# Sampling distances of a deformable convolution made by GpSimd instead of VectorE

## What is computed

```
out = conv2d(x, conv1_w, conv1_b); out = relu(batchnorm(out, ...))
offset = conv2d(out, off_w, off_b)              # 18 maps: y and x for 9 taps
py = off[:, :, 0] + ky + oy;  px = off[:, :, 1] + kx + ox
sampled = v00*w00 + v01*w01 + v10*w10 + v11*w11   # bilinear, zero outside the image
out = einsum('bckhw,ock->bohw', sampled, w) + b
```

## Time and profile before

| | us |
|---|---|
| median of 3 runs (lowest, highest) | 107.54 (107.26, 108.07) |
| the profiled execution | 107.54 |
| its span, first to last instruction | 105.4 |
| PE busy in the span | 93.1 (88%) |
| DVE busy | 68.5 (65%) |
| ACT busy | 48.4 (46%) |
| POOL busy | 29.9 (28%) |
| products on DVE (line 666), 21 instructions | 20.9 |

### The profile page before, as it was taken

One profiled execution on the slowest core, in us unless ns is written; L12 is line 12 of the kernel. 1 busy time (PEld: TensorE's weight loads), 2 busy tenths in 40 slices (PEclk: granted clock), 3 DMA queues, 4 the chain that ended last, 5 costly groups with the idle time before them and its releaser, 6 DMA issues.

```text
span 105.4 us, 3065 instructions
## 1 busy us (share of the span) xinstructions
PE 93.1 (88%) x1280; PEld 67.1 (64%) x1280; DVE 68.5 (65%) x186; ACT 48.4 (46%) x96; POOL 29.9 (28%) x43
## 2 busy tenths in 40 slices
PE   5979995796496999999978899999999999996970
PEld 2346641485375777777733889989899745583940
DVE  6655974239999998399335455655556569759451
ACT  5655812308989999756526990000000015651120
POOL 3000916910000004999880000000000006285510
PEclk9999999999999999999999999999999999999999
DMA  2899999999100000000000000000000000000001
GB/s 72 233 346 382 213 190 202 200 191 217 50 3 6 0 0 3 6 0 0 0 6 0 0 6 0 6 0 6 0 6 0 0 6 3 0 0 6 0 0 50
DMA packets 4589, 6.35 MB, mean 60 GB/s; under 512 B 512, under 2 KB 3840, under 8 KB 4576
## 3 DMA queue, kind: packets, MB, share of 16 engines
q1 hardware_dynamic: 4576, 6.16, 24.9%
HBM read 6.03 MB, written 0.13 MB: 58 GB/s over the span
## 4 chain that ended last, share of the span: by engine, by line
PE 70%; DVE 17%; DMA 4%; ACT 3%; issue 3%; SPq 1%; DVEq 0%; ACTq 0%
PE ps L1041 23%; PE ps L961 13%; PE ps L972 8%; DVE st L666 6%; PE ps L854 5%; DMA taps<-in_taps 4%; PE ps L1156 3%; PE ps L834 3%; PE ps L1054 2%; PE ps L913 2%; DVE hats L643 1%; PE ps L898 1%; DVE prodt L790 1%; PE ps L1149 1%; PE ps L1088 1%
## 5 line engine op out<-in xcount | busy, mean ns | idle before, releaser
L666 DVE TENSOR_TENSOR st<-hats 128x1024 f32<-128x1024 f32 (+1 forms) x21 | 20.9, 1043 | 2.2 <-PE ps L961 2.2
L961 PE MATMUL ps<-ident,st 128*128 128x128 f32 x144 | 17.9, 276 | 2.3 <-DVE st L666 2.3
L507 ACT ACTIVATE s<-ps 128x512 f32<-128x512 f32 x33 | 17.3, 601 | 4.5 <-PE ps L961 4.5
L961 PEld LDWEIGHTS ps<-ident,st 128*128 128x128 f32 x144 | 15.6, 141 | 5.9 <-DVE st L666 3.4
L834 PE MATMUL ps<-zeros 128*128 128x512 bf16 x53 | 13.9, 413 | 1.9 <-DVE zeros L576 1.2
L439 ACT ACTIVATE std<-mv,par 128x1 f32<-128x1 f32 x4 | 1.2, 295 | 27.4 <-DVE mv L564 27.4
L1041 PE MATMUL ps<-yt,wband 128*64 128x96 f32 (+1 forms) x240 | 12.3, 259 | 0.5 <-DVE yt L700 0.5
L1041 PEld LDWEIGHTS ps<-yt,wband 128*64 128x64 f32 x240 | 11.4, 136 | 1.5 <-issue 0.7
L1041 PE MATMUL ps<-ytb,wband 128*64 128x96 f32 (+1 forms) x240 | 12.2, 259 | 0.1
L1041 PEld LDWEIGHTS ps<-ytb,wband 128*64 128x64 f32 x240 | 11.3, 136 | 0.9 <-DVE ytb L715 0.2
L834 PEld LDWEIGHTS ps<-zeros 128*128 128x128 bf16 x53 | 5.2, 104 | 8.6 <-issue 1.9
(11 more groups left out here) (177 smaller groups left out, 121.6 us busy)
## 6 DMA issues: line engine op xcount, KB each, us to landing
wband<-in_wb SPq DMA_DIRECT2D x4, 720.0 KB, 14.5
wa<-in_wa SPq DMA_DIRECT2D x1, 576.0 KB, 7.0
taps<-in_taps SPq DMA_DIRECT2D x1, 560.0 KB, 5.1
taps<-in_taps SPq DMA_DIRECT2D x1, 448.0 KB, 4.0
wa<-in_wa SPq DMA_DIRECT2D x1, 324.0 KB, 5.4
wc<-in_wc SPq DMA_DIRECT2D x1, 256.0 KB, 15.5
cst<-in_cst SPq DMA_DIRECT2D x1, 242.0 KB, 5.4
sel<-in_sel SPq DMA_DIRECT2D x1, 192.0 KB, 4.3
```

Source lines behind the costliest of these rows:

```text
L507: a.activation(s[:, k % 2, kb, 2 * pair:2 * pair + 2, :], ps[:, turn_bank(e), :], ACT.Copy).then_inc(drained_a, 1)
L666: v.tensor_tensor(st[:, k % 2, half, low:low + count, :].rearrange("p b (y x) -> p b y x", x=W), view(hats[:, half, k, low, 0:1], (16, cou ...
L961: last = t.transpose(ps[:, turn_bank(e), HW * i + P * half:HW * i + P * half + P], st[:, k % 2, half, 2 * pair + i, P * kb:P * kb + P], id ...
```

## The change

The distances of groups 1 to 4 leave VectorE's stream. GpSimd makes them one behind the other, with the same operands and shapes, as soon as `pos_ready` is signalled and its fills are done. The order of everything else stays.

```
@@ gpsimd
             g.wait_ge(band_zeroed, 6)
+            g.wait_ge(pos_ready, 1)
+            for c in range(1, len(HAT_GROUPS)):
+                dist, grid = distances(c)
+                g.tensor_tensor(hat_group(c), dist, grid, ALU.subtract).then_inc(dist_ready, 1)
@@ vector
-            def distance(c):
-                dist, grid = distances(c)
-                v.wait_ge(pos_ready, 1)
-                v.tensor_tensor(hat_group(c), dist, grid, ALU.subtract).then_inc(dist_ready, 1)
-
@@ vector
                 for pair in range(2):
                     for half in range(2):
                         multiply(k, half, 2 * pair, 2)
-                    if k == 0:
-                        distance(pair + 1)
             for k in range(PAIRED_TAPS, TAPS):
-                if k == 2:
-                    distance(3)
-                if k == 4:
-                    distance(4)
                 for half in range(2):
```

## The result

| | median us | runs | ratio to before (95% interval) |
|---|---|---|---|
| before | 107.79 (107.26 to 108.07) | 4 | |
| changed | 111.03 (110.60 to 111.23) | 4 | 1.030 (1.027 to 1.033) |

A forecast was written before the change was run, and what follows sets the result against it. VectorE bounds the kernel until tap 2's transposes, then TensorE. Holds of 3.4 us and a 0.6 us wait for group 2's hats move those transposes from 33.14 to 35.45: 107.54 + 2.3 = 109.9 us, range 108.6 to 112.1.

The forecast's parts named there:

- What bounds it: Around the sampling: VectorE until 33.09 us, then TensorE; the end moves as the start of tap 2's transposes (33.14) moves.
- What is taken away: Distances of groups 1 to 3, 1.58 us on VectorE's path; even free on GpSimd they gain only 0.41 us.
- The hold: VectorE beside GpSimd's four distances: held for each one's time less its tail, 3.4 us for 2048 elements.
- The lower bound of the forecast: VectorE's hold at the fast end: 619 ns less a fixed 0.3 over 256 elements, 1.25 ns each, 2.5 us.
- The rival of short holds: Each distance holds VectorE for only 0.31 us, 1.24 in all; 107.7 us, chance 0.10.
- The whole instruction as a lock: Rival: VectorE is held for all of each GpSimd distance, 4.3 us with starts and tails; 110.8 us, chance 0.10.
- Where the four fall: All four holds fall before tap 0's fourth product, alternating with products; it ends at 29.99 instead of 26.93 us.
- What is late next: Behind tap 0: transposes, drain, group 2's hats, 3.05 us; VectorE waits 0.6, tap 2's transposes start 2.3 us later.
- TensorE's pace: Rival: TensorE, idling in tap 0, falls to 1.2 GHz at 30.0 us; put at 111.8 us, chance 0.14.
- The half-way case of that rival: TensorE's pace falls at 30.0 us but is back half-way to tap 2: 111.1 us.
- the forecast's own range: Whole-kernel time, 108.9 to 111.2 us, from hold bounds of 2.5 and 4.7 us; forecast's chance 0.60.
- the wider range: Whole-kernel time, 108.6 to 112.1 us, leaving out two lower rivals and the upper end of the pace rival.

The follow-up runs named there:

- e2_beside: Kernel before, all distances on VectorE, plus the four subtractions made again by GpSimd into a tile nobody reads: 111.40 us, 1.032.
- e3_filler: Changed kernel with 12 filler matmuls of 512 columns on TensorE in the gap before tap 0's transposes: 109.92 us, 1.022.
- e6_copies: Changed kernel with GpSimd copying the positions (one input) in place of subtracting the grid (two inputs): 108.17 us, 1.004.
- e8_last_only: Kernel before with only group 4's distance moved to GpSimd, right behind the positions: 108.72 us, 1.008.
- e1_fills: Changed kernel with GpSimd's four subtractions replaced by fills of the same sizes, which write and read nothing from SBUF: 107.22 us, 0.994.
- e7_few_fillers: Changed kernel with 4 filler matmuls on TensorE before tap 0's transposes: 110.84 us, 1.026.
- e5_regroup: Kernel before, distances on VectorE reordered, group 3's hats later, taps 4 to 8 regrouped as (4, 5) and (6, 7, 8): 107.34 us, 0.995.

## Why the prediction was right, and where it was short

- **What bounds it.** Right. TensorE is full from tap 2 on in both traces (21.21 of 21.30 us), and the loss in the stage (3.0) is nearly the loss in the time (3.2), as in the other slower kernels (e2, e3, e6 and e8, by the medians): +3.4 and +3.6, +2.2 and +2.1, +0.4 and +0.4, +0.8 and +1.0.
- **What is taken away is worth little.** Right, and somewhat low: 0.41 us forecast for the stage, 0.5 measured there (0.6 in the time) where the distances cost VectorE nothing (e1_fills).
- **The hold, the step that decides.** Right. 3.4 us forecast; measured are 7.80 - 4.91 = 2.89 on the products and 0.39 on tap 0's hats (0.68 for 0.29), 3.3 us together, 1.6 ns an element. The forecast's rule, a distance's own time less its tail, comes out in each of the four: 3.8 us of their own less four tails of 0.12 to 0.15. e2_beside shows that reads beside reads do it whatever tile they go to, e1_fills that writes alone don't, and e6_copies that instructions with one input hold for half of what those with two do. The lower bound of the forecast rested on a fixed 0.3 us of a GpSimd instruction, which no row shows; a copy of 4 elements took 0.19 in all (line 388 of before), and by that the bound would be 1.7 ns an element, not 1.25. The rival of short holds (0.31 us each) took the scaling's number for one of its instruction; it was one of its 384 elements with one input, and with 512 or 768 elements and two inputs it grows.
- **The whole instruction as a lock.** As a mechanism this rival was closer than its price. Subtractions and copies hold VectorE for all of their own time but the last 0.12 to 0.15 us; its 110.8 came from 4.3 us of GpSimd time, where 3.8 were measured. The Trainium skill (SBUF — State Buffer, "Who interferes with whom") has the exclusion right, down to a fill that doesn't take part in it (e1_fills); on the length its whole instruction is too long by that tail here, and by 0.7 us for the scaling of before.
- **Where the four fall.** The sum was right and the order was not. The forecast let the first product run ahead of distance 2. In the trace distance 2 is issued at 24.75, before the first product at 24.98, because tap 0's hats were held too; so distances 2 and 3 both fell ahead of the end of the second product. The last product of tap 0 ends 6.35 us behind the positions, and 29.99 - 23.53 = 6.46 were forecast. But TensorE idles for 3.3 us and then for 1.0, instead of twice for about 2.
- **What is late next.** Right: the chain through transposes, last drain and group 2's hats sets tap 2, and VectorE waits for it. At full pace (e3_filler) this wait is 0.64 us, with 0.6 forecast.
- **TensorE's pace.** This is where the forecast is short. It was a rival with 0.14, set aside with the words that each gap is about 2 us with work on both sides. It happened, and for less than its price: 1.1 us in the time (111.03 to 109.92), where 111.8 for 109.9 was given, since the level was back at 33.5, before tap 1's transposes. The half-way case of that rival, 111.1, is what came out. The argument against it doesn't hold: in e7_few_fillers the gap is 2.44 us, and the clock falls. That rival also read a low level from the slow first fillers; the granted clock of that trace stands at 1.00 there, so those rows alone don't show one. That the lower level doubles a transpose is shown by the changed kernel (eight in 1.97 us for 1.09). So the missing term of the sum is 0.8 us in the stage: from the first of the eight transposes to tap 2's first product are 3.81 us in the changed kernel (30.43 to 34.24) and 2.99 at full pace (e3_filler, 30.09 to 33.08).
- **The number.** 111.03 lies inside the forecast's own range (108.9 to 111.2), which was made from the bounds of the hold alone. The hold was 3.3 us, near its middle, and a term that the sum did not have brought the time close to the upper end. That the own range still held it is luck; the wider range had the rival of the pace in it.

What stays open: when the clock falls. The mean granted clock was low in every execution of the kernels with gaps of 3.3 and 2.44 us, and in some executions of e3_filler, e6_copies and e8_last_only but not in others of the same program. The runs change gap and work around it together.

## What to carry to other kernels

Moving a two-input instruction from VectorE to GpSimd doesn't take it off VectorE while VectorE itself works out of SBUF: here four subtractions, of which VectorE had paid 1.6 us on its path, held it for 3.3 us from the other engine. Look in the trace of before for a VectorE instruction that lasts longer beside a GpSimd one; the excess is the price of a move, and it is best taken from an instruction of the same kind, since a scaling held VectorE for less than a third of its own time and a subtraction for nearly all of it. Then look at what the longer wait does to TensorE's clock, for that is a second price, and ask what is next behind the path that is shortened: here ScalarE, a few tenths of a microsecond away, and these tenths were to be had by reordering and regrouping the distances on VectorE (e5_regroup).

## What the runs showed of the hardware

- A GpSimd instruction that reads SBUF holds up VectorE instructions with two SBUF inputs: subtractions with two inputs for about 1.6 ns an element (3.3 us for 2048), copies with one input for 0.7 ns (e6_copies, 1.5 us for 2048). It lets VectorE go 0.12 to 0.15 us before its own end, the scaling of before 0.8 us before it. Fills hold the products up by nothing, and one tensor_scalar by 0.07 us at most (e1_fills). Where both engines have instructions waiting, they alternate, one by one (the rows of the changed kernel above).
- VectorE's own hats, a tensor_scalar of 256 elements with one input in SBUF, was held in the same way: 0.68 us (changed) and 1.11 us (e8_last_only) for 0.29.
- In the trace of e7_few_fillers TensorE's level fell to 1.2 GHz behind an idle gap of 2.44 us, with 0.8 us of fillers before it, and stayed there for nearly 7 us (about 28.5 to 35.3) while TensorE was mostly busy. The same program can run with and without a fall: e3_filler took 109.4 to 110.0 us in four executions at a mean clock of 0.993 or more, and 110.9 and 111.0 in two at 0.984.
